# Wide attentions: the values of a step as two stacked products and four bands, and a new order on ScalarE

## The reference, cut to what matters

```python
x = x + _L2_xattn_ref(_layernorm(x, axis=-1), ctx_768, Wq, Wk, Wv, Wo, bo)
...
        q = x @ Wq
        k = context @ Wk
        v = context @ Wv
        sim = jnp.einsum('bhid,bhjd->bhij', q, k) * SCALE
        attn = jax.nn.softmax(sim, axis=-1)
        out = jnp.einsum('bhij,bhjd->bhid', attn, v)
        return out @ Wo + bo
```

## Time and profile before

| | us |
|---|---|
| median of 3 runs (3553.38 to 3579.91) | 3554.26 |
| profiled execution | 3553.97 |
| its span, first to last instruction | 3552.1 |
| busy in the span: PE 96%, PEld 79%, DVE 70%, ACT 57%, POOL 35% | |
| mean granted TensorE clock, share of full speed | 0.988 |

### The profile page before, as it was taken

How to read it: one execution, slowest core, us unless ns; L and a number is a source line. 1 busy time by engine, 2 the same in 40 slices (tenths; PEclk the granted TensorE clock), 3 DMA queues, 4 the chain that set the end, 5 groups by cost and what they waited for, 6 DMA issues and landing times. The chain is left out here.

```text
span 3552.1 us, 99744 instructions
## 1 busy us (share of the span) xinstructions
PE 3412.4 (96%) x43493; PEld 2808.9 (79%) x43493; DVE 2473.8 (70%) x4946; ACT 2033.0 (57%) x3467; POOL 1244.1 (35%) x923
## 2 busy tenths in 40 slices
PE   7999899999999899999999989999999998999999
PEld 6888788887888555788888878878888886777777
DVE  8977555555667799666666667766666666777776
ACT  4445555554666688455555545555555555566564
POOL 1322133334554233222222223322222224555555
PEclk9999999999999999999999999999999999999999
DMA  3000000001000000000000000010000000000000
GB/s 110 11 11 11 1 1 1 1 1 38 15 15 8 1 1 1 23 9 7 7 9 7 5 22 1 1 47 9 7 7 9 7 5 1 7 7 13 7 7 13
DMA packets 15488, 41.03 MB, mean 12 GB/s; under 512 B 2959, under 2 KB 4687, under 8 KB 14158
## 3 DMA queue, kind: packets, MB, share of 16 engines
q1 hardware_dynamic: 15054, 34.64, 3.2%
HBM read 30.44 MB, written 4.19 MB: 10 GB/s over the span
## 5 line engine op out<-in xcount | busy, mean ns | idle before, releaser
L708 ACT ACTIVATE projL<-bank 128x512 f32<-128x512 f32 (+1 forms) x640 | 371.3, 601 | 646.0 <-PE bank L291 630.4
L511 POOL TENSOR_TENSOR probL<-probL,invL 128x1024 f32<-128x1024 f32 x160 | 304.5, 1903 | 1196.5 <-DVE invL L821 1196.5
L1704 POOL TENSOR_TENSOR h_loM<-hM,h_hiM 126x512 fp32r<-126x512 f32 x224 | 290.3, 1296 | 254.7 <-ACT h_hiM L1830 252.0
L598 PEld LDWEIGHTS bank<-valuesL,probTL 64*64 64x64 f32 x10240 | 277.7, 133 | 60.9 <-issue 55.0
L810 DVE TENSOR_REDUCE neg_maxL<-bank 128x16 f32<-128x1024 f32 x160 | 195.9, 1224 | 183.7 <-PE bank L617 152.9
L598 PE MATMUL bank<-valuesL,probTL 64*64 64x128 f32 x10240 | 316.4, 272 | 4.4 <-ACT probTL L718 4.4
L1403 PEld LDWEIGHTS bank<-w2T,hM 128*128 128x128 f32 x2304 | 276.8, 192 | 39.3 <-ACT hM L1458 24.1
L1403 PE MATMUL bank<-w2T,hM 128*128 128x128 f32 x2304 | 283.4, 276 | 16.2 <-ACT hM L1458 16.2
L1458 ACT ACTIVATE hM<-bank,ahead_scales 128x512 f32<-128x512 f32 x288 | 183.8, 684 | 189.3 <-PE bank L291 189.0
L825 DVE COPY valuesL<-bank 128x512 f32<-128x512 f32 x320 | 213.1, 679 | 107.2 <-PE bank L291 101.3
L818 DVE TENSOR_REDUCE totalL<-probL 128x16 f32<-128x1024 f32 x160 | 194.8, 1217 | 122.4 <-ACT probL L723 122.1
(11 more groups left out here) (309 smaller groups left out, 9050.0 us busy)
## 6 DMA issues: line engine op xcount, KB each, us to landing
ct0L<-in_ctxP SPq DMA_DIRECT2D x24, 192.0 KB, 2.5
ct1L<-in_ctxP SPq DMA_DIRECT2D x24, 192.0 KB, 2.5
x<-in_x SPq DMA_DIRECT2D x4, 1024.0 KB, 10.9
out<-x SPq DMA_DIRECT2D x8, 512.0 KB, 2.6
nct<-in_ctxP SPq DMA_DIRECT2D x16, 192.0 KB, 2.4
ahead_second<-in_L0w SPq DMA_DIRECT2D x2, 1152.0 KB, 18.1
ahead_second<-in_L3gate SPq DMA_DIRECT2D x1, 882.0 KB
ahead_second<-in_L3up SPq DMA_DIRECT2D x1, 882.0 KB
```

The source lines that it names most:

```text
L511: nc.gpsimd.tensor_tensor(segments(prob[:, slot, :]), segments(prob[:, slot, :]), per_segment(inv[:, slot, :]), ALU.mult).then_inc(prob_re ...
L598: last = nc.tensor.matmul(o_bank[b * SEQ:(b + 1) * SEQ, t, u * D:(u + 1) * D], probT[t * SEQ:(t + 1) * SEQ, 2 * s + u, b * SEQ:(b + 1) * SEQ],
L708: nc.scalar.activation(proj[:, u, :], rot.bank(step, f"P{u}")[0:rows, :], ACT.Copy, scale=scale if paired and u % 2 == 0 else 1.0).then_in ...
L1704: nc.gpsimd.tensor_tensor(h_lo[:, a % SLOTS, :], h[:, a % 3, :], h_hi[:, a % SLOTS, :].bitcast(F32), ALU.subtract).then_inc(lo_ready, 1)
```

## The change

The 288 rows of a value's three products are packed anew. `T1` holds the context's high part (96 rows) and the low part of rows 0 to 31; `M1` holds M_hi and again its rows 0 to 31. `T2` holds the high part of rows 0 to 63 and the low part of rows 32 to 95; `M2` holds M_lo of rows 0 to 63 and M_hi of rows 32 to 95. So `value` is two matmuls of 128 rows. What is left, the high part of rows 64 to 95 against M_lo, is 32 rows: `T3` holds it for the four token tiles in four bands of 32 partitions, `M3` holds four copies of the weights, and `values_rest` issues four matmuls of 32 rows at the end of the values of a step, one into each of the four banks. V_done of all four values comes only from these.

The host lays out three forms of the context (ctxA, ctxB, ctxC), which are loaded by three DMAs for each group instead of one. `split_context` becomes `stack_context`: five POOL operations in L0, six in L2 and L3, in place of two, one of them on 128 columns. `keep_rest(r)` on DVE becomes eight operations on 512 columns instead of one; in L2 and L3 those of r = 2 and 3 move from before the first step into the steps k = 1 and 2 of group 0. There PE waits for `stack_kept`. V0 of a group (k == 0) waits for the whole of `stack_context`; before, P0 waited for the split context.

On ACT the exponential moves behind T1, P2 and P3, to just before V0. On DVE `split_transposed` moves ahead of `totals`. `values` has three slots instead of four.

```diff
@@ -419,7 +421,7 @@
-        M_hi, M_lo = (sb(f"M{n}{tag}", [K, heads, D], F32R) for n in ("_hi", "_lo"))
+        M1, M2, M3 = (sb(f"M{n}{tag}", [P, heads, D], F32R) for n in (1, 2, 3))
@@ -428,21 +430,24 @@
-        ct = [sb(f"ct{s}{tag}", [K, GT]) for s in range(2)]
-        ct_hi, ct_lo = ([sb(f"ct{n}{s}{tag}", [K, GT], F32R) for s in range(2)] for n in ("_hi", "_lo"))
+        raw = [[sb(f"ct{n}{s}{tag}", [P, cols]) for n, cols in (("A", GT), ("B", GT), ("C", P))] for s in range(2)]
+        T1, T2 = ([sb(f"T{n}{s}{tag}", [P, GT], F32R) for s in range(2)] for n in (1, 2))
+        T3 = [sb(f"T3{s}{tag}", [P, P], F32R) for s in range(2)]
+        ct_lo = [sb(f"ct_lo{s}{tag}", [K, GT], F32R) for s in range(2)] if paired else None
-        values = sb(f"values{tag}", [P, 4, 4, 4, D])
+        values = sb(f"values{tag}", [P, 3, 4, 4, D])
-        fold_bank = (c.bank[1], c.bank[2], c.bank[3], c.bank[7]) if paired else (c.bank[1], c.bank[3])
+        fold_bank = c.bank[0:4] if paired else (c.bank[1], c.bank[3])
+        parts = 6 if paired else 5
-        folded, hi_kept, lo_kept = sem("folded"), sem("hi_kept"), sem("lo_kept")
+        folded, hi_kept, lo_kept, stack_kept = sem("folded"), sem("hi_kept"), sem("lo_kept"), sem("stack_kept")
@@ -485,7 +490,13 @@
-                first_contexts(sp, c, "ctxP", ct, ct_in)
+                def load_context(j):
+                    for dst, name in zip(raw[j % 2], ("ctxA", "ctxB", "ctxC")):
+                        cols = dst.shape[1]
+                        sp.dma_start(dst[:, :], dram[name][:, j * cols:(j + 1) * cols]).then_inc(ct_in[j % 2], 16)
+                load_context(0)
+                load_context(1)
@@ -496,15 +507,39 @@
-                later_contexts(sp, c, "ctxP", ct, ct_in, S_done, Q, 0)
+                for j in range(2, NG):
+                    sp.wait_ge(S_done, (j - 1) * Q)
+                    load_context(j)
-                for j in range(2):
-                    split_context(nc, pool, c, ct, ct_hi, ct_lo, j, j, 0, ct_in, ct_split)
+                def stack_context(j, slot):
+                    A, B, C = raw[slot]
+                    pool.wait_ge(ct_in[slot], 48 * (j // 2 + 1))
+                    def high_part(part, high):
+                        nc.gpsimd.tensor_tensor(high[:, :], part[:, :], c.one[:, :].to_broadcast([P, part.shape[1]]), ALU.mult)\
+                            .then_inc(ct_split, 1)
+                    high_part(A, T1[slot])
+                    if paired:
+                        pool.wait_ge(ct_split, parts * j + 1)
+                        nc.gpsimd.tensor_tensor(ct_lo[slot][:, :], A[0:K, :], T1[slot][0:K, :].bitcast(F32), ALU.subtract)\
+                            .then_inc(ct_split, 1)
+                    high_part(B, T2[slot])
+                    high_part(C, T3[slot])
+                    for n, (part, high, rows) in enumerate(((A, T1[slot], slice(96, P)), (B, T2[slot], slice(64, P)))):
+                        pool.wait_ge(ct_split, parts * (j + 1) - 2 + n)
+                        nc.gpsimd.tensor_tensor(high[rows, :], part[rows, :], high[rows, :].bitcast(F32), ALU.subtract)\
+                            .then_inc(ct_split, 1)
+                    pool.wait_ge(ct_split, parts * (j + 1))
+                stack_context(0, 0)
+                stack_context(1, 1)
@@ -516,7 +551,7 @@
-                            split_context(nc, pool, c, ct, ct_hi, ct_lo, i + 1, 1 - slot, turn, ct_in, ct_split)
+                            stack_context(i + 1, 1 - slot)
@@ -544,13 +579,13 @@
-                    pe.wait_ge(lo_kept, 2 * rounds)
+                    pe.wait_ge(lo_kept, rounds)
-                    ct_parts = ct_hi[slot][:, :], ct_lo[slot][:, :]
+                    ct_parts = (T1[slot][0:K, :], ct_lo[slot][:, :]) if paired else None
@@ -563,11 +598,19 @@
+                    heads_of = slice(4 * k, 4 * k + 4)
-                    weights = tuple(M[:, 4 * k:4 * k + 4, :].rearrange("p h d -> p (h d)") for M in (M_hi, M_lo))
-                    product(nc, rot.bank(step, f"V{u}")[:, :], (ct_hi[slot][:, tok], ct_lo[slot][:, tok]), weights)\
-                        .then_inc(V_done, 1)
+                    for n, (tokens, weights) in enumerate(((T1, M1), (T2, M2))):
+                        nc.tensor.matmul(rot.bank(step, f"V{u}")[:, :], tokens[slot][:, tok],
+                                         weights[:, heads_of, :].rearrange("p h d -> p (h d)"), start=(n == 0), stop=False,
+                                         skip_group_check=True)
+                def values_rest(slot, k, step):
+                    for u in range(4):
+                        band = slice(32 * u, 32 * u + 32)
+                        nc.tensor.matmul(rot.bank(step, f"V{u}")[:, :], T3[slot][band, :],
+                                         M3[band, 4 * k:4 * k + 4, :].rearrange("p h d -> p (h d)"), start=False, stop=True,
+                                         skip_group_check=True).then_inc(V_done, 1)
@@ -629,9 +672,10 @@
-                            pe.wait_ge(ct_split, 2 * i + 2)
+                        if k == 0 and paired:
+                            pe.wait_ge(ct_split, parts * i + 2)
@@ -647,8 +691,10 @@
-                        if m == 0 and paired:
-                            pe.wait_ge(lo_kept, 6)
+                        if k == 0:
+                            pe.wait_ge(ct_split, parts * (i + 1))
+                        if i == 0:
+                            pe.wait_ge(stack_kept, k + 1)
@@ -658,8 +704,11 @@
+                        values_rest(slot, k, step)
+                        if paired and i == 0 and k in (0, 2):
+                            pe.wait_ge(stack_kept, k + 2)
-                            output(n, back[0], back[1], bstep % 4)
+                            output(n, back[0], back[1], n % 3)
@@ -730,9 +779,6 @@
-                        if k or started(i, 1):
-                            exponentials(m - 1, (step - 1) % 2)
-                        if older:
@@ -741,6 +787,8 @@
+                        if k or started(i, 1):
+                            exponentials(m - 1, (step - 1) % 2)
@@ -774,18 +822,34 @@
+                def keep_low_queries(r):
+                    hs = slice(r * 4, (r + 1) * 4)
+                    dve.wait_ge(hi_kept, 2 * r + 1)
+                    nc.vector.scalar_tensor_tensor(out=A_lo[:, hs, :].rearrange("p h k -> p (h k)"),
+                                                   in0=c.bank[2 * r][:, 0:4 * K], scalar=scale,
+                                                   in1=A_hi[:, hs, :].bitcast(F32).rearrange("p h k -> p (h k)"),
+                                                   op0=ALU.mult, op1=ALU.subtract).then_inc(lo_kept, 1)
+                def flat(M, rows, r):
+                    return M[rows, r * 4:(r + 1) * 4, :].rearrange("p h d -> p (h d)")
+                def stack_copies(r):
+                    dve.wait_ge(hi_kept, r + 3 if paired else 2 * r + 2)
+                    for M, to, rows in ((M1, slice(96, P), slice(0, 32)), (M2, slice(64, 96), slice(32, 64)),
+                                        (M2, slice(96, P), slice(64, 96))):
+                        nc.vector.tensor_copy(flat(M, to, r), fold_bank[r][rows, :])
+                def stack_differences(r):
+                    nc.vector.tensor_tensor(flat(M2, slice(0, 64), r), fold_bank[r][0:64, :],
+                                            flat(M1, slice(0, 64), r).bitcast(F32), ALU.subtract)
+                    for u in range(4):
+                        last = nc.vector.tensor_tensor(flat(M3, slice(32 * u, 32 * u + 32), r), fold_bank[r][64:96, :],
+                                                       flat(M1, slice(64, 96), r).bitcast(F32), ALU.subtract)
+                    last.then_inc(stack_kept, 1)
-                    hs = slice(r * 4, (r + 1) * 4)
-                    if not paired:
-                        dve.wait_ge(hi_kept, 2 * r + 1)
-                        nc.vector.scalar_tensor_tensor(out=A_lo[:, hs, :].rearrange("p h k -> p (h k)"),
-                                                       in0=c.bank[2 * r][:, 0:4 * K], scalar=scale,
-                                                       in1=A_hi[:, hs, :].bitcast(F32).rearrange("p h k -> p (h k)"),
-                                                       op0=ALU.mult, op1=ALU.subtract).then_inc(lo_kept, 1)
-                    dve.wait_ge(hi_kept, r + 3 if paired else 2 * r + 2)
-                    nc.vector.tensor_tensor(M_lo[:, hs, :].rearrange("p h d -> p (h d)"), fold_bank[r][0:K, :],
-                                            M_hi[:, hs, :].bitcast(F32).rearrange("p h d -> p (h d)"), ALU.subtract)\
-                        .then_inc(lo_kept, 1)
+                    stack_copies(r)
+                    stack_differences(r)
@@ -794,15 +858,17 @@
-                keep_rest(0)
-                keep_rest(1)
-                if paired:
-                    keep_rest(2)
-                    keep_rest(3)
+                    keep_rest(0)
```

(18 more changed lines are left out.)

8 lines of the change are left out of this document (4 added, 4 removed).

## The result

The changed kernel takes 3595.28 us (median of 8, 3589.66 to 3616.55), the kernel before 3553.82: a ratio of 1.0111, with an interval of 1.0091 to 1.0131. The prediction was 3549 with a range from 3500 to 3592. The profiled execution took 3600.18 us, 46.2 more than that of before.

The account below looks back on a forecast made before the run. PE was taken to bound L0, L2 and L3, with DVE close behind in L0. From 3553.97, L2 and L3 gave -4.8 each and L0 +5: 3549.4, so 3549, with a range of 3500 to 3592.

Parts of the forecast that it names:

- the values: PE's values in each step: four bands run concurrently, so V gets 0.55 us shorter.
- Rivals 2 and 4: 2: bands run one after another, 3612, chance 0.10; 4: the bands' weight loads queue, 3576, chance 0.06.
- The order on ACT: Exponential moved behind P3's copy: costs nothing, with 1.4 us of cover before multiply's transposes.
- POOL's stack: In L2 and L3, 6.8 us of POOL work delays DVE in k = 2; PE waits 1.3 us a group.
- d: DVE's delay in k = 2 from waiting for POOL's operations: 2.5 us, the middle of 1.75 and 3.25.
- rival 1: DVE slips through POOL's gaps or is late by 1.2 only, no group stalls: 3496 to 3502, chance 0.28.
- the slack: DVE's spare time in L2 and L3 until PE transposes x in k = 3: 1.2 us.
- The starts: Start of L2 and L3: longer keep_rest, 5.5 us for each r, puts PE 10 us behind in each phase.
- L0: Whole phase L0, start and steps: 5 us more, between 6 less and 14 more.
- The chain round the stack: L0, from V0 through projections, exponential, totals, multiply and stack: 21.5 us for two steps, against 22.2 before.
- Rival 3: Exclusion at its worst, d = 3.25, and L0 bound by DVE and POOL: 3585 to 3594, chance 0.10.

Follow-up runs that it names:

- experiment 1: Changed kernel with POOL's stack moved from step k = 1 to k = 0: 3510.72 us, ratio 0.9859 to the kernel before.
- 5: Kernel before with its split of the context moved from k = 1 to k = 0: 3553.07 us, ratio 0.9982.
- 6: Changed kernel with the stack in k = 0 and the exponential back between the copies of T0 and T1: 3561.47 us, ratio 1.0019 to the kernel before.
- 8: Kernel before with only the exponential moved behind P3's copy on ACT: 3592.35 us, ratio 1.0090.
- 12: Kernel before with the exponential behind P3's copy and split_transposed ahead of totals, without stack or new values: 3561.26 us, ratio 0.9991.
- experiment 4: Changed kernel with the exponential back in its old place on ACT, DVE's order kept new: 3572.83 us, ratio 1.0029 to the kernel before.
- experiment 2: Changed kernel with the DVE operation that ACT's square root waits for put ahead of both keep_rest: 3580.57 us, ratio 1.0057 to the kernel before.
- experiment 7: Kernel before with four idle POOL operations behind each context split and the exponential behind P3's copy: 3608.42 us, ratio 1.0142.

## Why the prediction was wrong, point by point

**What bounds it, and the values: right.** V fell by 0.50 (forecast 0.55), a step by 0.47. Rivals 2 and 4 fell with the first timeline. Experiments 1 and 5 together show the gain: with the context's work in k = 0 in both kernels the change, its two new orders included, is worth 1.2%, though its longer starts are still in it. Without the new order on ACT it is worth nothing (6).

**The order on ACT: zero, right only for both orders together and without the stack.** I looked only at ACT's copies and the date of `multiply`. Alone the exponential's move costs 0.9% (8); the change's second order, on DVE, which I didn't price at all, pays it back (12), and that is luck. The slack that I gave it for the transposes was real, but DVE's x of the next group was nearer. Beside the stack in k = 1 it isn't zero either: without the exponential's move the changed kernel is 0.8% faster (1.0029 against 1.0111, experiment 4).

**POOL's stack: the step that failed.** The forecast made of it a stall of 1.3 us a group, from DVE's delay d = 2.5 less a slack of 1.2. Measured were 2.07, and 0.65 more for the clock. The stack's length (6.8 forecast, 6.5 measured), its start and its end were right. The terms behind it were wrong. d is 2.95, where I took the middle of 1.75 and 3.25: the middle had no row behind it, and DVE hardly ever slips through, which is also the end of rival 1. In L2's later groups of the changed kernel a normalisation takes 0.97 in the median, against 0.34 in experiment 1:
```profile
L220 DVE TENSOR_SCALAR xh<-x,stats,rstd x60: 335/966/1457, 1521.7 to 2067.8; 128x128 f32<-128x128 f32 x60
```
Then the slack: I let it end at the transposes of x, and called the banks hidden. PE was stopped earlier, at P1, for V1's bank, and again at T0. Of the stall of 2.07 k = 3 gives back 0.2. The Trainium skill ("SBUF — State Buffer", section "SBUF: two separate sides") says that a GpSimd operation and a DVE operation in a two-port mode, or with two SBUF inputs, lock a shared port pair, and that the one that comes second blocks for the whole instruction. The rows agree in both directions: 4.07 for four normalisations, and POOL's 3.46 against DVE's 2.57 in L0.

**The clock: a term that I didn't have.** I put a clock's fall into the starts only. In the groups it makes k = 3 9.87 on average instead of 9.22 in L2, 0.65 for each of 14 (0.57 in L3). A group was to gain 0.9. In the profile it gains 4 x 0.47 = 1.9, loses 1.85 in the stall and 0.65 to the clock, so it loses 0.6. That is 1.5 us off in each of 28 groups, some 42 of the 51 us between the forecast's sum, 3549.4, and the profiled 3600.2. Without the stall both go: 36.4 us for a group in experiment 1, against 38.35 before.

**The starts: the mechanism right, the size at its bound.** `keep_rest` takes 5.6 (forecast 5.5). The first maxima came 8.6 and 6.6 later and the first group took 4.6 more, 13.2 and 11.2 against 10. What I missed is the root: ACT's queue was named nowhere in that part, though its wait of 5.1 us stood behind DVE's 16 operations. Moving one operation gives 7 us of the two starts back (2).

**L0: near in the sum (+8 against +5), by luck.** Two errors nearly cancel. The chain round the stack was forecast at 21.5 for two steps; they took 21.07 in the later groups. The loss is in groups 2 to 7, where the quantisation holds POOL up and V0 waits: four distances from the maxima of k = 0 to those of k = 1 are 13.6 to 15.8 instead of 10.6. I had +2 for it. What the place of the stack kept from L0 (20 us) I saw only in experiment 1.

**The rivals.** Rival 3, exclusion at its worst, had 3585 to 3594 and a chance of 0.10. Its number is the nearest to the measured 3595, but in part by luck. Its stall of 2.05 is right to 0.02, though from a d of 3.25 and with the wrong waits in it. It had 14 for L0, where 8 came, and nothing for the clock, where 17 us came in L2 and L3.

What stays open: why the clock falls in k = 3 of some groups only, and of fewer in experiment 2; what lets P1 pass in experiment 7; and what L0 loses with ACT's late exponential in 12.

## What to carry to other kernels

When a transformation moves work from the engine that bounds the kernel to another, ask at what date that work runs and which instructions of a neighbour share something with it: here moving the same POOL operations from one step to the one before it was worth 2.5%. A move in one engine's order is to be followed through every queue behind it; the exponential's move shifted POOL's work by 2 us into DVE's busiest stretch. And a wait on PE is to be priced with the clock that it may cost, here a third on top.

## What was not expected of the hardware

- A change between full products and one band of 32 rows costs 0.10 us for the first full product behind it (0.33 instead of 0.23), and a lone band takes 0.43 until the next product, just as four do.
- The exclusion works against POOL too: a subtraction of 1.28 us took 3.46 beside a DVE operation of 2.57 on SBUF. DVE's copies from PSUM, its reductions and its subtraction from PSUM kept their 0.61 and 1.22 beside POOL (experiment 1, k = 0).
- The granted clock fell in k = 3 after stalls of 2 us in 11 of 28 groups, though PE was busy for 588 of 613 us in L2; after stalls of 0.9 us (experiment 7) it fell in none.
